# Expert stage in 72 blocks of 128 slots, rows sent as fp16 halves, its ends laid over both halves of attention

## The reference, cut to what matters

```python
xn = layernorm(x)                                  # x: 8 x 512 tokens of 128
s  = attention(xn, W_qkv, W_out)                   # 32 query heads, 16 key heads of 64, causal, alibi bias
logits = xn @ gate_w + gate_b                      # 8 experts
topk_w = softmax(top2(logits)); comb = sum(onehot * topk_w)
h = gelu(xn @ w1[e] + b1[e])                       # 128 -> 512
y = h @ w2[e] + b2[e]                              # 512 -> 128
out = x + s * silu(sum_e y[e] * comb[e])
```

## Time and profile before

| | us |
|---|---|
| median of 3 runs (1262.40 to 1267.58) | 1265.14 |
| profiled execution, its own time | 1268.53 |
| its span, first to last instruction | 1266.8 |
| PE busy | 1172.2 (93%) |
| DVE, ACT, POOL busy | 1031.9, 935.6, 876.9 |

### The profile page before, as it was taken

One profiled execution on the slowest core, in us unless ns is written; L12 is line 12 of the kernel. 1 busy time (PEld: TensorE's weight loads), 2 busy tenths in 40 slices (PEclk: granted clock), 3 DMA queues, 4 the chain that ended last, 5 costly groups with the idle time before them and its releaser, 6 DMA issues.

```text
span 1266.8 us, 54444 instructions
## 1 busy us (share of the span) xinstructions
PE 1172.2 (93%) x17690; PEld 925.5 (73%) x17691; DVE 1031.9 (81%) x3180; ACT 935.6 (74%) x1759; POOL 876.9 (69%) x1080
## 2 busy tenths in 40 slices
PE   1589999999999999997999889999999999999992
PEld 0457777777777777776888757777777777777772
DVE  8878888888888888874888768888888888888874
ACT  1458888888888888874666568888888888888882
POOL 9168888888888888882000058888888888888883
PEclk9979999999999999998999989999999999999996
DMA  6436666666666666672222337655555555555663
GB/s 219 161 79 143 141 149 142 142 142 142 141 141 142 141 142 142 141 136 55 81 83 83 89 88 133 141 133 133 133 133 133 133 133 133 133 133 133 136 121 85
DMA packets 266626, 162.75 MB, mean 128 GB/s; under 512 B 154466, under 2 KB 255170, under 8 KB 265924
## 3 DMA queue, kind: packets, MB, share of 16 engines
q1 hardware_dynamic: 262468, 153.54, 52.5%
q0 software_dynamic: 4096, 8.40, 2.5%
HBM read 18.91 MB, written 16.78 MB: 28 GB/s over the span
## 4 chain that ended last, share of the span: by engine, by line
PE 84%; DVE 6%; SPq 4%; issue 2%; DMA 2%; ACT 1%; POOL 1%; DVEq 0%; ACTq 0%
PE ps L783 11%; PE ps L809 11%; PE ps L711 9%; PE ps L712 8%; PE ps L713 8%; PE ps L813 6%; PE outs L840 6%; PE outs L844 6%; PE outs L842 6%; PE ps L810 4%; PE ps L792 3%; PE ps L816 2%; DVE mix L1143 1%; PE outs L711 1%; PE outs L712 1%
## 5 line engine op out<-in xcount | busy, mean ns | idle before, releaser
L675 POOL TENSOR_TENSOR h<-stage 128x512 f16<-128x512 f32 x640 | 656.2, 1040 | 118.1 <-ACT stage L1034 109.0
L1197 DVE CUSTOM_DVE_ANT_0 stage<-ps,kmask 128x512 f32<-128x512 f32 (+3 forms) x1024 | 462.7, 488 | 117.2 <-PE ps L783 108.0
L1034 ACT ACTIVATE stage<-ps,slope 128x512 f32<-128x512 f32 (+1 forms) x768 | 453.9, 617 | 133.1 <-PE ps L816 97.5
L809 PE MATMUL ps<-q_st,k_st 128*128 128x256 f16 (+3 forms) x1024 | 306.0, 301 | 2.1 <-DMA q_st<-stage 1.7
L840 PE MATMUL outs<-v_sp,stage 128*128 128x65 f16 x2560 | 283.6, 194 | 4.5 <-DVE stage L1227 4.0
L844 PE MATMUL outs<-v_sp,h 128*128 128x65 f16 x2560 | 283.3, 193 | 0.0
L842 PE MATMUL outs<-v_sp,stage 128*128 128x64 f16 x2560 | 283.1, 193 | 0.0
L783 PE MATMUL ps<-k_st,stage 128*128 128x512 f16 (+3 forms) x1024 | 246.5, 302 | 9.5 <-DVE spread L1197 5.7
L840 PEld LDWEIGHTS outs<-v_sp,stage 128*128 128x128 bf16 x2560 | 237.8, 97 | 15.2 <-issue 5.0
L842 PEld LDWEIGHTS outs<-v_sp,stage 128*128 128x128 bf16 x2560 | 235.1, 98 | 9.4
L844 PEld LDWEIGHTS outs<-v_sp,h 128*128 128x128 f16 x2560 | 234.8, 97 | 0.0
(11 more groups left out here) (196 smaller groups left out, 2815.1 us busy)
## 6 DMA issues: line engine op xcount, KB each, us to landing
k_st<-stage SPq DMA_DIRECT2D x256, 128.0 KB
q_st<-stage SPq DMA_DIRECT2D x256, 128.0 KB, 2.4
q_st<-stage SPq DMA_DIRECT2D x256, 64.0 KB, 2.1
k_st<-stage SPq DMA_DIRECT2D x128, 64.0 KB
stage<-slot_x SPq DMA_DIRECT2D x40, 128.0 KB, 2.0
slot_y<-stage SPq DMA_DIRECT2D x40, 128.0 KB, 1.7
slot_x<-att SPq DMA_DIRECT2D x2, 2048.0 KB, 8.7
wx_raw<-in_L_ffn_w SPq DMA_DIRECT2D x64, 64.0 KB, 1.9
```

The source lines that it names most:

```text
L675: pool.tensor_tensor(t_lo[r], t_p[r], upper(t_p[r]), ALU.subtract).then_inc(s[f"lo{u % NG}"], 1)
L809: pe.matmul(d, k[:, 0, at], q[:, 0, seen], start=True, stop=False, skip_group_check=True)
L1034: e = act.activation(t_p[r][:, c0:c1], S_ps[u % 2][:, c0:c1], ACT.Exp, scale=slope[:, bass.ds(pair_index(n) * 2 * SLOTS + sl * 2 + h, 1)])
L1197: ins = dve.tensor_tensor_reduce(junk[h][:, c0:c0 + w], M_ps[h][:, c0:c0 + w], kmask[:, SEQ - w:SEQ], -1.0 / 1024, 3e38, ALU.add, ALU.min, ...
```

## The change

- Blocks have 128 slots. There are 72 of them (before: 40 of 256), in 18 steps of four, with four buffers each.
- The rows are sent as fp16 halves: ACT makes the high one (`send_hi`, new task R0), POOL the low one (`send_ready`). They take 512 bytes as before. SP loads a block with a transposing DMA straight into `xgT`, so PE's transposes, ACT's and DVE's halves of the rows go.
- `hidden` has four chunks of three matmuls with 128 columns, `down` four chunks of three. PE runs three blocks ahead with `hidden`, loads an expert register for every block, and addresses the weights as before.
- ACT makes four gelus of 128x128 a block; DVE makes the halves in 128x512 pieces, one pair a block, and one output copy of 128x128.
- The stage's first blocks overlap the last body's end: `LATE_O` puts the last output projections between blocks. During the last 20 blocks (from step 13) `begin_half` puts the early tasks of the second half between blocks, on every engine.
- The buffers h32, h_hi and h_lo now lie over X, so X is loaded again (4 DMAs of 512 KB) after the stage.
- `ORDER` of both halves is written anew, with a position for each task; K0 and Q0 are two bodies ahead.

```diff
-BLK = 256
+BLK = P
 NBLK = (2 * TOK + E * (BLK - 1)) // BLK
-NBLK += NBLK % 2
-BT = BLK // P
+NBUF = 4
+NBLK += -NBLK % NBUF
+STEPS = NBLK // NBUF
+FILL_FROM = 13
...
+            def load(j, c):
+                block_done(sp, "hmm", j, c - NBUF)
+                sp.dma_start_transpose(xgT[:, c % NBUF, :, :], slot_x[bass.ds((j * NBUF + c) * BLK, BLK), :])\
+                  .then_inc(s[f"xload{c % NBUF}"], 16)
+            def store(j, c):
+                block_done(sp, "yout", j, c)
+                sp.dma_start(slot_y[bass.ds((j * NBUF + c) * BLK, BLK), :], y_sb[:, c % NBUF, :])\
+                  .then_inc(s[f"ystore{c % NBUF}"], 16)
...
+            for c in range(NBUF):
+                load(0, c)
+            leave_bodies("SP", {**stacks, "W": load_weights}, 0, HALF)
+            with sp.Fori(0, FILL_FROM) as i_:
+                for c in range(NBUF):
+                    load(i_, c + NBUF)
+                    store(i_, c)
+            for j in range(FILL_FROM, STEPS):
+                for c in range(NBUF):
+                    if j < STEPS - 1:
+                        load(j, c + NBUF)
+                    store(j, c)
+                    begin_half("SP", stacks, HALF, BODIES, (j - FILL_FROM) * NBUF + c)
+            for c in range(4):
+                sp.dma_start(X[:, 8 * c:8 * c + 8, :], xt[:, 8 * c:8 * c + 8, :]).then_inc(s["xend"], 16)
...
+            def hidden(j, c, e):
+                block_done(pe, "xload", j, c, 16)
+                block_done(pe, "gelu", j, c - 2)
+                x_hi, x_lo = xgT[:, c % NBUF, 0, :], xgT[:, c % NBUF, 1, :]
+                for f in range(FC):
+                    w = bass.ds(e * FC + f, 1)
+                    mm = three(S_ps[c % 2][:, f * P:(f + 1) * P], wx_hi[:, w, 0, :].rearrange("p a d -> p (a d)"),
+                               wx_lo[:, w, 0, :].rearrange("p a d -> p (a d)"), x_hi, x_lo)
+                mm.then_inc(s[f"hmm{c % NBUF}"], 1)
+            def down(j, c, e):
+                y = O_ps[c % 2][:, 0:D]
+                block_done(pe, "yout", j, c - 2)
+                pe.matmul(y, ones[:, :], b2_row[:, bass.ds(e, 1), :].rearrange("p a d -> p (a d)"),
+                          start=True, stop=False, skip_group_check=True)
+                block_done(pe, "hlo", j, c)
+                for f in range(FC):
+                    w, cols = bass.ds(e * FC + f, 1), slice(f * P, (f + 1) * P)
+                    mm = three(y, h_hi[:, c % NBUF, cols], h_lo[:, c % NBUF, cols],
+                               wx_hi[:, w, 1, :].rearrange("p a d -> p (a d)"),
+                               wx_lo[:, w, 1, :].rearrange("p a d -> p (a d)"),
+                               start=False, stop=(f == FC - 1), shared_bank=True)
+                mm.then_inc(s[f"ymm{c % NBUF}"], 1)
+            def step_of(j, c):
+                if not isinstance(j, int) or j * NBUF + c + 3 < NBLK:
+                    pe.reg_load(expert[(c + 3) % NBUF], blk_expert[0:1, bass.ds(j * NBUF + c + 3, 1)])
+                    hidden(j, c + 3, expert_of((c + 3) % NBUF))
+                down(j, c, expert_of(c % NBUF))
...
+            def gelus(j, c):
+                k = c % NBUF
+                e = act.value_load(blk_expert[0:1, bass.ds(j * NBUF + c, 1)], min_val=0, max_val=E - 1)
+                block_done(act, "hmm", j, c)
+                block_done(act, "hlo", j, c - NBUF)
+                for f in range(FC):
+                    cols = slice(f * P, (f + 1) * P)
+                    ins = act.activation(h32[:, k, cols], S_ps[c % 2][:, cols], ACT.Gelu,
+                                         bias=b1T[:, bass.ds(e * FC + f, 1)], scale=1.0 / WS)
+                ins.then_inc(s[f"gelu{k}"], 1)
...
+            with dve.Fori(2, FILL_FROM) as i_:
+                for c in range(NBUF):
+                    parts(i_, c)
+                    outputs(i_, c - 2)
```

More of the change, by code:

```diff
@@ L267, in build @@
         s = {n: sem("s_" + n) for n in names}
+        for step in ("xload", "hmm", "gelu", "hhi", "hlo", "ymm", "yout", "ystore"):
+            for k in range(NBUF):
+                s[f"{step}{k}"] = sem(f"s_{step}{k}")
         for step in ("scored", "exp", "lo", "valued"):
@@ L296, in build, with one_window @@
         bodies_of_half = [0, HALF]
-        def one_window(engine_name, tasks, w, lo, hi, phase):
-            for name, off in ORDER[lo // HALF][engine_name]:
+        def one_window(engine_name, tasks, w, lo, hi, phase, late=(), part=None):
+            table = ORDER[lo // HALF][engine_name]
+            for name, off, at in table:
                 n = w + off
-                if name[0] not in tasks or (isinstance(w, int) and not lo <= n < hi):
+                if name[0] not in tasks or name == "O0" and n in late or (isinstance(w, int) and not lo <= n < hi):
                     continue
                 if isinstance(w, int) and n == lo and name in AHEAD[engine_name]:
+                    continue
+                if part is not None and at * part[1] // 100 != part[0]:
                     continue
@@ L327, in run_bodies, with leave_bodies, begin_half, block_done @@
                     one_window(engine_name, tasks, i_ * UNROLL + c, lo, hi, c)
-            for w in range(end, hi + 2):
+            for w in range(end, hi):
                 one_window(engine_name, tasks, w, lo, hi, w)
+        def leave_bodies(engine_name, tasks, lo, hi, late=()):
+            for w in (hi, hi + 1, hi + 2):
+                one_window(engine_name, tasks, w, lo, hi, w, late)
+        LATE_O = [w + next(off for name, off, _ in ORDER[0]["PE"] if name == "O0") for w in (HALF, HALF + 1, HALF + 2)]
+        LATE_O = [n for n in LATE_O if n < HALF]
+        def begin_half(engine_name, tasks, lo, hi, b):
+            bodies_of_half[:] = lo, hi
+            blocks = (STEPS - FILL_FROM) * NBUF
+            names = AHEAD[engine_name]
+            for i, name in enumerate(names):
+                if i == b:
+                    tasks[name[0]](lo, lo % UNROLL, int(name[1:]))
+            b -= len(AHEAD["PE"])
+            each = (blocks - len(AHEAD["PE"])) // 2
+            if b >= 0:
+                one_window(engine_name, tasks, lo - 2 + b // each, lo, hi, lo + b // each, part=(b % each, each))
+        def block_done(eng, step, j, c, each=1):
+            need(eng, f"{step}{c % NBUF}", (j + c // NBUF + 1) * each)
         stage_of = [stage[:, i, :] for i in range(NSTG)]
@@ new lines, in _ @@
+            for c in range(3):
+                pe.reg_load(expert[c], blk_expert[0:1, c:c + 1])
+                hidden(0, c, expert_of(c))
+            for sl in range(SLOTS):
+                pe.wait_ge(s[f"al{sl}"], HALF)
+            for j in range(2):
+                for c in range(NBUF):
+                    step_of(j, c)
+                    if (j, c) == (0, 1):
+                        for n in LATE_O[:-1]:
+                            project(n, n % UNROLL, 0)
+                    if (j, c) == (1, 1):
+                        for n in LATE_O[-1:]:
+                            project(n, n % UNROLL, 0)
@@ L891, in _ @@
+            with pe.Fori(2, FILL_FROM) as i_:
+                for c in range(NBUF):
+                    step_of(i_, c)
             for j in ("00", "01", "10", "11"):
@@ L1056, in _ @@
             go_ahead("ACT", tasks, 0, HALF)
[L1057 removed]
+            enter_bodies("ACT", {**tasks, "W": weights_hi, "R": send_hi}, 0, HALF)
             weights_split(act)
@@ L1102, in _ @@
+            act.preload_act_table(ACT.Gelu)
+            with act.Fori(0, FILL_FROM) as i_:
+                for c in range(NBUF):
+                    gelus(i_, c)
+            for j in range(FILL_FROM, STEPS):
+                for c in range(NBUF):
+                    gelus(j, c)
+                    begin_half("ACT", tasks, HALF, BODIES, (j - FILL_FROM) * NBUF + c - 2)
+            for c in (2, 3):
+                begin_half("ACT", tasks, HALF, BODIES, (STEPS - 1 - FILL_FROM) * NBUF + c)
             act.preload_act_table(ACT.Exp)
-            enter_bodies("ACT", {**tasks, "F": weigh}, HALF, BODIES)
@@ L1104, in _ @@
-            for r in range(2):
-                act.wait_ge(s[f"ystore{r}"], NBLK // 2 * 16)
             run_bodies(act, "ACT", {**tasks, "F": weigh}, HALF, BODIES)
+            leave_bodies("ACT", {**tasks, "F": weigh}, HALF, BODIES)
             act.wait_ge(s["added"], NT)
@@ new lines, in _ @@
+            with dve.Fori(2, FILL_FROM) as i_:
+                for c in range(NBUF):
+                    parts(i_, c)
+                    outputs(i_, c - 2)
+            for j in range(FILL_FROM, STEPS):
+                for c in range(NBUF):
+                    parts(j, c)
+                    outputs(j, c - 2)
+                    begin_half("DVE", tasks, HALF, BODIES, (j - FILL_FROM) * NBUF + c - 2)
+            for c in (2, 3):
+                outputs(STEPS - 1, c)
+                begin_half("DVE", tasks, HALF, BODIES, (STEPS - 1 - FILL_FROM) * NBUF + c)
```

307 lines of the change are left out of this document (96 added, 211 removed), and 40 rows, old and new, of the table ORDER.

## The result

The changed kernel takes **1377.24 us** (median of 4 runs, 1376.33 to 1378.60) beside 1266.36 (4 runs, 1262.40 to 1267.92) of the kernel before: ratio **1.088**, 95% interval 1.085 to 1.091. The forecast was 1323 with a range up to 1372. The direction is right, and in the expert stage the mechanism too; the loss is 111 us, not 57, and 24 us of what is missing lie in the second half of attention, where the forecast had a small gain.

A forecast was written before the change was run, and what follows sets the result against it. It took PE's instruction queue to bound the expert stage and the array to bound attention: 1268.5 + 61.5 - 4 = 1326 us for the profiled execution, 1323 as median, range 1284 to 1372.

The forecast's parts named there:

- The new address: Expert stage, PE's queue: each group of three matmuls takes a new weight address, 0.25 us; eight groups a block, 2.00.
- the register load: Expert stage, PE's queue: loading the next block's expert, 0.34 us of hole plus 0.17 of matmuls, taken as 0.50 a block.
- the clock: Expert stage: full array clock assumed; a rival had it fall to 1.2 GHz, 3.4 us a block, 1357 us; chance 0.05.
- rival one: Expert stage: PE's queue hides address work, a block takes 1.73 us, in all 1243 us; chance 0.15.
- The ring: Expert stage: loads wait behind stores, 2.7 us a block, hidden; as rival 3.1 to 3.6, 1337 to 1371 us, chance 0.12.
- sum of 221.8 for the seams: From half one's last values to half two's first scores: 221.8 us in all, against 160.3 before, so +61.5.
- The block: Expert stage: PE needs 2.90 us a block of 128 slots, bounds 2.65 and 3.3; 68 steps make 197.2.
- waits on counts: Expert stage, PE: four waits a block on counts that depend on the loop, between 0 and 0.4 us, taken as 0.13.
- Late projections: Start of the expert stage: three late output projections between blocks, 1.5 us each, 4.6 in all.
- Early tasks and SP's stacking: Last blocks of the stage: half two's early tasks add 3 us, SP's stacking DMAs delaying loads add 5.
- the new `ORDER`: Both attention halves: array time unchanged, taken as -2 us, range -12 to +10.
- The reload: After the stage: loading X again, 4 x 512 KB, is hidden if stacks aren't late, 0 us, up to +6.

The follow-up runs named there:

- the loads first: The changed kernel with the load of block b+5 issued ahead of the store of block b: 1404.95 us in one run, 1407.67 in another.

## Why the prediction was right and wrong

**Right.** The new address at 0.25 us (0.26 in the timeline), the register load at 0.50 (0.50), the clock, and rival one's failure: the addresses aren't hidden. The ring was forecast at 2.7 and hidden. It is hidden, but by luck in part: only by some 0.3 us in two blocks, at about 3.0 (an estimate, above); 2.56 was measured only where PE's own work in it was gone. The Trainium skill's page "TensorE: Matmul & The Clock Gate", section "Wait — 56ns, not 53.3ns?", gives 55.6 ns from start to start for 128 columns. The rows agree where no new address stands between two matmuls (692.97 to 693.02 above); where one does, the changed kernel's starts are 0.09 to 0.13 apart. One such step lies inside each group of three and not behind it, as the low part of the weight has a register operation of its own.

**The 54 us between forecast and result:** the stage 19, the second half 24 (with the forecast's whole -4 set against it), the first half 7, and 4 because I set the median 3 below the profiled execution where it lay 1 above.

**Where the sum of 221.8 for the seams fell short by 19.**
- The ramp: the first step ended 10.2 us after the last values, forecast 8.1: +2.
- The block: 3.10 to 3.13 instead of 2.90, over 68 steps +15. The term that was mis-sized is what I had guessed at 0.13 for waits on counts and 0.14 for the loop: 0.27 together, where the measured block leaves 3.10 - 2.63 = 0.47 beside the sum's other terms. Every fourth block takes 3.4, the others 3.0: the turn is 0.1 a block. The rest I put down to waits: the raw records have four on PE a block, as I had counted, and the one that stands by itself takes 0.11 us of the queue, so about 0.4 (an estimate), the upper end of what I had allowed them; no run takes them off. The bounds (2.65 to 3.3) held it.
- Late projections: 4.6 forecast, about 1 measured (25.5 for the eight blocks that they are in; eight at 3.10 are 24.8). Their addresses are known ahead, which would let the queue pass them quickly; no run tests that.
- Early tasks and SP's stacking: 3 + 5 forecast, 58.8 - 16 x 3.10 = 9 measured, and 3 with the loads first.
- The last three steps without `hidden` and the first scores: 3.9 forecast, 8.8 measured from the start of block 69. I counted only their matmuls; with nothing else to do PE waits there for gelu and halves of each block.

**Wrong outside the stage.** I gave both halves together -4, and the first took +7.0 and the second +20.4, the largest miss. The failed step is the sentence on the new `ORDER`: "array time is unchanged; holes between matmuls are at most a few tenths in a body of 15.8". Its range ended at +10, and the order took 13.6. The hole at the loop's turn, 1.03 us from start to start where nothing is queued, costs 0.7 us every second body, and I had read no turn in the trace of before, where PE's starts at it are 0.22 apart; in the changed kernel's first half, with the turn behind a query, they are 0.21. The reload was mis-sized by 5.6 because I costed its bytes and not its place on SP's queue. The first half, +7.0, had no term but its share of the order's: its first scores came 1.0 later, the first body took 23.3 instead of 18.8 us, and the others 15.79 instead of 15.75. Why the first body is longer, no run shows.

**What I saw without using it.** The block of before was 3.02 of array and "most of 0.34" of queue; I added them up. They are two bounds, 3.00 and 3.20, that lie nearly on each other. Read that way, the queue's work for one block of the new kernel could have been read off the old block directly: the same addresses, the same register, so at most about 3.2, instead of 2.90 from single prices.

## What to carry to other kernels

Before tiles are made smaller, count what PE's queue does for one tile (register loads, data-dependent addresses, waits on counts), because that didn't shrink with the tile here (3.20 and 3.10 us); when blocks are addressed by data, the block should be as large as the array time needs to cover it. A busy share of 97% doesn't say which of array and queue is the bound: take one off and see, or look whether the starts within a group keep their distance while the holes between groups grow. Keep the turn of a loop behind long queued matmuls, and count every DMA put on a queue by what stands behind it.

## What the runs showed that I had not expected

- In the raw records an address by a register is two register operations on PE's queue, one for the high and one for the low part of the weight, 0.147 and 0.113 us apart; with three matmuls of 56 ns under it, it shows, with three of 109 it doesn't. The record of the register load takes 0.30 us, and the next starts 0.36 after it.
- A transposing load of 64 KB takes 1.17 us of SP's issue, a plain store of the same size 0.34; behind three or four stacks it took 1.26 to 1.30, and twice 1.75, once of these with no stack ahead of it.
- One and the same text of the first half has PE's starts 0.4 to 0.6 us apart at fixed places of a body in some runs and in none of these places in others, on the same chip, where another kernel of equal work moves by under 1%.
